# A perceiver layer on one core: half of the sort keys move from VectorE to GpSimd, and ScalarE's row copies are placed anew

## The chip, the cores and the metric

The kernel runs on one core of one Trainium2 chip. The metric is the device time of one execution in microseconds; the time given is the median of three runs.

## The reference

A perceiver layer: cross attention of 4 x 256 query rows to 4 x 4096 context rows (256 columns, 16 heads of 16), then a gated attention with a running sum, then a feed-forward part in 4-bit floating point. What is changed lies in the cross attention, in the focus and the sparsifying of queries and keys:

```python
def _focus(x, f):
    x = jnp.abs(jnp.where(x >= 0, x, 0.01 * x)) + 1e-6
    nrm = x.mean(axis=-1, keepdims=True)
    return jax.nn.softmax(jnp.log(x) * f, axis=-1) * nrm

def _topk_sparsify(x):               # rows of 16 values, one head each
    _, idx = jax.lax.top_k(jnp.abs(x), 11)
    return x * mask_of(idx)          # the other 5 become 0
...
q, k = _focus(q @ Wq.T, f), _focus(k @ Wk.T, f)
qh, kh = _topk_sparsify(heads(q)), _topk_sparsify(heads(k))
z_inv = einsum('bnd,bd->bn', qh, kh.mean(axis=1)) + 1e-6
kv = einsum('bnc,bnd->bcd', kh / 64, vh / 64)
y = einsum('bnc,bcd->bnd', qh, kv) / z_inv[..., None]
```

Every row of 256 values is thus projected, made positive, raised to a power, normalised, and in each of its 16 heads the 5 smallest of 16 values are set to zero. Ties go by position, as top_k has them.

## The kernel before

**Groups.** The rows are worked on in groups of 1024: 128 partitions by T = 8 tiles of 256 columns, 2048 elements in a partition. Group 0 is the queries, groups 1 to 16 are the context, four for each batch. After group 0 the work goes by pairs of groups: `pairs_of_groups` (L298) calls `pair(a, last)` for a = 1, 3, ... 15 on each of three engines; b = a + 1 is the second group of the pair, c = a + 2 and d = a + 3 are the groups of the next pair. Each engine runs its own written-out order of steps, and semaphores tie them.

**One group's way.** TensorE transposes the context rows (`context_turn` L779, `transpose_quad` L739, matmuls on L745) in four quads of two tiles. ScalarE copies each quad out of PSUM to `rows_T` (`rows_to_sbuf` L471, activation on L422), and TensorE projects it (`project` L764, L772). ScalarE's `lift` (L461, L467) makes the value positive and adds up the row; two tiles each time, four times a group. The columns lie by position first: columns 16j to 16j + 15 are position j of the 16 heads. VectorE's `make_keys` (L1200, L1203) makes a sort key of each lifted value: an integer operation clears the lowest four bits and writes the order of the position there, with `key_and` and `key_xor` (L1179 to L1185). Then it finds the fifth smallest key of each head by a network of minima and maxima: `compare_pairs` (L1224), `sort_fours` (L1238, which also gives the row maximum `rowmax`, L1250), `find_fifths` (L1257). `make_mask` (L1281, L1286) compares all keys with it. Meanwhile ScalarE takes the logarithm of the lifted values in place (`logarithms` L480, L484), which must wait until the keys are made, and the exponentials (`exponentials` L486, L501), which need the row maximum. VectorE multiplies by the mask (`apply_mask` L1215, L1219) and makes the row scale (L1221); ScalarE scales (`scale_rows` L507, L513), and TensorE sums products with the context rows (`sum_group` L858, L866).

**Buffers.** `focus_words` holds six planes of a group: two lifted (also the logarithms), two key planes, two of exponentials; each is taken by group number modulo 2. So the keys of group c go where those of group a were, and may not before `make_mask(a)` is done. There is one `mask`. TensorE has two banks for transposed quads and four for projections.

**Order of VectorE in a pair** (L1317): `compare_pairs(a)`, `sort_fours(a)`, `make_keys(b)`, `compare_pairs(b)`, `sort_fours(b)`, `find_fifths` of both, `make_mask(a)`, `inverse_sums(a)`, `apply_mask(a)`, `make_mask(b)`, `make_keys(c)`, `inverse_sums(b)`, `apply_mask(b)`. The last pair has an order of its own, with `make_keys(b)` in the same place.

**Order of ScalarE in a pair** (L524): logarithms of a, copies 0 and 1 of c, exponentials of a, logarithms of b, (in every second pair `save_sums`), then exponentials of b in two halves with the row copies and lifts of c and d between and behind them, `scale_rows(a)` ahead of the last two lifts of d, and `scale_rows(b)` last.

**Order of TensorE in a pair** (L873): turns 0 and 1 of c, the sums of the group before a, then projections and turns of c and d by turns, then the sums of a.

**GpSimd** (L357) makes constants at the start, a maximum over partitions at L389, and splits the biases of the gated attention (L403, L405, L408). After that it has nothing to do. **SP** issues the context loads (L312).

Of the kernel before, what the change touches and what calls it, by code (L numbers as in the profile page):

```python
# [18 lines left out]
P = 128  # L19
F32 = mybir.dt.float32  # L20
BF16 = mybir.dt.bfloat16
I32 = mybir.dt.int32
I16 = mybir.dt.int16
ALU = mybir.AluOpType
# [5 lines left out]
HEADS, HD = 16, 16  # L30
HIDDEN = 1024
# [13 lines left out]
FP4_MAX, FP8_MAX = 6.0, 448.0  # L45
TINY = 1e-20
# [17 lines left out]
def perceiver_layer(nc, x, ctx, Wq, Wk, Wv, Wp, focus, W_qkv, b_qkv, W_gate, b_gate,  # L64
# [9 lines left out]
    with es:  # L74
# [48 lines left out]
        key_xor = sb("key_xor", [P, D], I32)  # L123
# [9 lines left out]
        key_and = sb("key_and", [P, 1], I32)  # L133
        key_flip = sb("key_flip", [P, 1], I32)
        key_base = sb("key_base", [P, 1], I32)
# [100 lines left out]
        keyed = sem("keyed")  # L236
        logs_done = sem("logs_done")
# [58 lines left out]
        LAST_QUAD = AFTER_QUAD + len(TAIL_QUADS)  # L296

# [112 lines left out]

        @block.scalar
        def _(act):
# [67 lines left out]
            def logarithms(n, s):  # L480
                act.wait_ge(lifted_ready, PAIRS * n + PAIRS)
                act.wait_ge(keyed, n + 1)
                logs = lifted[(s + 1) % 2]
                act.activation(logs, logs, ACT.Ln, bias=EPS).then_inc(logs_done, 1)  # L484
# [39 lines left out]
            def pair(a, last):  # L524
# [18 lines left out]
                else:  # L543
                    exponentials(b, at(b), FORE_TILES)
                    rows_to_sbuf(c, 2)
                    lift(c, 0, at(c))
                    exponentials(b, at(b), HIND_TILES)
                    rows_to_sbuf(c, 3)
                    lift(c, 1, at(c))
                    lift(c, 2, at(c))  # L550
                    lift(c, 3, at(c))
                    rows_to_sbuf(d, 0)
# [508 lines left out]
        def _(dve):  # L1061
# [110 lines left out]
            for t in range(T):  # L1172
# [6 lines left out]
            step(dve.tensor_scalar(key_and[:, :], ff[:, :], 0.0, -float(HD), ALU.not_equal, ALU.mult))  # L1179
            step(dve.tensor_scalar(key_flip[:, :], ff[:, :], 0.0, -1.0, ALU.is_lt, ALU.mult))  # L1180
            then(dve.tensor_scalar(key_base[:, :], ff[:, :], 0.0, -1.0, ALU.is_equal, ALU.mult))
            step(dve.tensor_scalar(key_flip[:, :], key_flip[:, :], 0x7FFFFFF0, None, ALU.bitwise_and))
            then(dve.tensor_scalar(key_base[:, :], key_base[:, :], 0x3F800000, None, ALU.bitwise_and))
            then(dve.tensor_scalar(key_xor[:, :], order[:, :], key_base[:, 0:1], key_flip[:, 0:1],
                                   ALU.bitwise_xor, ALU.bitwise_xor))  # L1185
            step(dve.tensor_reduce(same_head[:, :], head_pick[:, :, :].rearrange("p m h -> p h m"), AX.X, ALU.add))
            def weight_max(w):
# [426 lines left out]
```

## Time and profile before

| what | value |
|---|---|
| median of 3 runs | 490.59 us (490.52 to 491.7) |
| the profiled execution | 490.7 us |
| its span, first to last instruction | 488.9 us |
| mean granted TensorE clock | 0.936 |
| busy: VectorE (DVE) / TensorE (PE) / ScalarE (ACT) / GpSimd (POOL) | 448.5 / 388.1 / 356.0 / 15.3 us |
| chain that ended last: VectorE / TensorE / issue / ScalarE | 68% / 16% / 9% / 4% |

In the profile DVE is VectorE, PE is TensorE's matmuls and PEld its weight loads, ACT is ScalarE, POOL is GpSimd. Times are microseconds from the start of the span; L numbers are lines of the kernel. A matmul's end is modelled, and the spans of GpSimd are rough. Groups of instructions name their output and input by the kernel's tensors; planes that lie in `focus_words` all carry that name.

### The profile page before, as it was taken

The page shows a single profiled execution, that of the slowest core. Times are in us where ns is not written, and L with a number is a line of the kernel's source. Part 1 is how long each engine was busy: PE and PEld are TensorE (multiplying, and loading weights), DVE is VectorE, ACT ScalarE, POOL GpSimd, SP SyncE. Part 2 cuts the span into 40 slices and gives each one's busy share as a digit, 9 for nine tenths or more (in the row PEclk, how much of TensorE's full clock was granted, in tenths as well). Part 3 has the DMA queues.
Part 4 walks back from the last instruction along what each step waited for, and adds up shares of the span by engine and source line. Part 5 has one row for each costly group of instructions (what it writes and reads, how often), then busy time and mean ns, then how long its engine had stood idle before and what let it go on. Part 6 is the DMA issues. An engine that isn't in the chain of part 4 may idle for free.

```text
span 488.9 us, 5944 instructions
## 1 busy us (share of the span) xinstructions
PE 388.1 (79%) x1877; PEld 300.9 (62%) x1880; DVE 448.5 (92%) x684; ACT 356.0 (73%) x937; POOL 15.3 (3%) x32
## 2 busy tenths in 40 slices
PE   1997749998988988988988898955999799554563
PEld 1876537777877877877777777855875345112232
DVE  4798999999999999999999999999988687989994
ACT  2569986897897887897887897855459466656643
POOL 4001420000000000000000000000000000000000
PEclk9998879999999999999999999985999999669976
DMA  7952000220220220220220220230200000000001
GB/s 235 359 181 86 0 1 1 87 86 2 86 86 2 86 87 1 87 86 1 87 86 1 86 86 1 62 112 0 87 0 0 1 1 1 0 0 0 23 21 43
DMA packets 27102, 27.65 MB, mean 57 GB/s; under 512 B 1216, under 2 KB 26816, under 8 KB 27072
## 3 DMA queue, kind: packets, MB, share of 16 engines
q1 hardware_dynamic: 26704, 27.27, 17.4%
q8 instruction: 15, 0.25, 0.2%
q14 instruction: 15, 0.12, 0.1%
q0 software_dynamic: 224, 0.01, 0.0%
q10 hardware_dynamic: 144, 0.00, 0.0%
HBM read 26.22 MB, written 1.05 MB: 56 GB/s over the span
## 4 chain that ended last, share of the span: by engine, by line
DVE 68%; PE 16%; issue 9%; ACT 4%; DMA 1%; SPq 0%; ACTq 0%
DVE focus_words L1219 8%; DVE focus_words L1203 8%; PE bank L944 5%; DVE sorted L1242 4%; DVE level L1228 4%; DVE level L1229 4%; DVE merge L1255 4%; DVE sorted L1243 4%; PE bank L772 3%; DVE sorted L1147 3%; DVE amax L1116 2%; DVE sorted L1248 2%; DVE sorted L1247 2%; DVE keymax L1245 2%; DVE merge L1253 2%
## 5 line engine op out<-in xcount | busy, mean ns | idle before, releaser
L772 PE MATMUL bank<-WkT,rows_T 128*128 128x256 f32 x512 | 127.0, 395 | 33.1 <-ACT rows_T L422 33.1
L772 PEld LDWEIGHTS bank<-WkT,rows_T 128*128 128x128 f32 x512 | 96.7, 197 | 50.6 <-ACT rows_T L422 38.8
L866 PE MATMUL bank<-ctx_words,focus_words 128*128 128x257 f32 x512 | 115.7, 384 | 4.9 <-ACT focus_words L513 4.9
L866 PEld LDWEIGHTS bank<-ctx_words,focus_words 128*128 128x128 f32 x512 | 99.8, 198 | 18.3 <-ACT focus_words L513 7.7
L501 ACT ACTIVATE focus_words<-focus_words,shift,ff 128x256 f32<-128x256 f32 x136 | 79.9, 591 | 0.6
L467 ACT ACTIVATE focus_words<-bank 128x256 f32<-128x256 f32 x136 | 50.0, 378 | 26.7 <-PE bank L772 26.7
L513 ACT ACTIVATE focus_words<-focus_words,row_scale 128x256 f32<-128x256 f32 x136 | 56.2, 508 | 11.6 <-DVE row_scale L1221 11.6
L422 ACT ACTIVATE rows_T<-bank 128x512 f32<-128x512 f32 x78 | 44.4, 595 | 23.5 <-PE bank L745 23.5
L1203 DVE SCALAR_TENSOR_TENSOR focus_words<-focus_words,key_and,key_xor 128x2048 int32<-128x2048 int32 x17 | 39.9, 2345 | 1.9 <-ACT focus_words L467 1.9
L745 PE MATMUL bank<-ident,ctx_words 128*128 128x128 f32 x256 | 38.4, 279 | 3.5 <-DMA ctx_words<-in_ctx_dram 2.9
L1286 DVE TENSOR_TENSOR mask<-focus_words,fifth 128x2048 bf16<-128x2048 f32 x17 | 39.0, 2292 | 0.5
L745 PEld LDWEIGHTS bank<-ident,ctx_words 128*128 128x128 f32 x256 | 31.6, 144 | 11.4 <-DMA ctx_words<-in_ctx_dram 5.2
L1219 DVE TENSOR_TENSOR focus_words<-focus_words,mask 128x2048 f32<-128x2048 f32 x17 | 38.6, 2268 | 0.0
L484 ACT ACTIVATE focus_words<-focus_words 128x2048 f32<-128x2048 f32 x17 | 32.4, 1909 | 0.0
L944 PE MATMUL bank<-WattT,rows_T 128*128 128x512 f32 x64 | 30.8, 603 | 0.0
L981 PE MATMUL bank<-gateT,focus_words 128*128 128x512 bf16 x30 | 13.4, 537 | 20.9 <-DVE ctx_words L1386 10.7
L467 ACT ACTIVATION_READ_ACCUMULATOR focus_words<-bank 128x1 f32 x136 | 27.7, 204 | 0.0
L501 ACT ACTIVATION_READ_ACCUMULATOR focus_words<-focus_words,shift,ff 128x1 f32 x136 | 25.8, 190 | 0.0
L745 PE MATMUL bank<-ident,focus_words 128*128 128x128 f32 x80 | 13.4, 307 | 12.2 <-DMA focus_words<-in_L_xattn_Wk_dram 9.5
L1242 DVE TENSOR_TENSOR sorted<-level 128x1024 f32<-128x1024 f32 x17 | 20.8, 1224 | 0.5
L646 ACT ACTIVATE ctx_words<-bank,out_scale 128x512 f32<-128x512 f32 x16 | 10.9, 686 | 14.3 <-PE bank L981 14.3
L1228 DVE TENSOR_TENSOR level<-focus_words 128x1024 f32<-128x1024 f32 x17 | 20.8, 1222 | 0.3
(187 smaller groups left out, 581.5 us busy)
## 6 DMA issues: line engine op xcount, KB each, us to landing
ctx_words<-in_ctx_dram SPq DMA_DIRECT2D x32, 512.0 KB, 3.9
ctx_words<-in_L_ffn_gate_w_dram SPq DMA_DIRECT2D x2, 1024.0 KB, 8.3
ctx_words<-in_L_ffn_up_w_dram SPq DMA_DIRECT2D x2, 1024.0 KB, 8.7
xs<-in_x_dram SPq DMA_DIRECT2D x4, 256.0 KB, 5.0
ctx_words<-in_L_ffn_down_w_dram SPq DMA_DIRECT2D x2, 512.0 KB, 9.5
ctx_words<-in_L_ffn_down_w_dram SPq DMA_DIRECT2D x1, 1024.0 KB, 4.8
out_dram<-xs SPq DMA_DIRECT2D x4, 256.0 KB, 2.1
focus_words<-in_L_attn_W_qkv_dram SPq DMA_DIRECT2D x1, 768.0 KB, 8.3
```

What stands on the lines that cost most here:

```text
L422: ins = act.activation(dst, src, ACT.Copy)
L467: ins = act.activation(lifted[(s + 1) % 2][:, t, :], proj_bank[m][:, (t % 2) * D:(t % 2 + 1) * D], ACT.Prelu, bias=NOT_ZERO, alpha=-0.01, ...
L501: ins = act.activation(expo[slot][:, t, :], lifted[slot][:, t, :], ACT.Exp, bias=shift[:, t:t + 1], scale=ff[:, 0:1], accum_out=exp_sum[:, ...
L513: ins = act.activation(expo[slot][:, t, :], expo[slot][:, t, :], ACT.Identity, scale=row_scale[:, slot, t:t + 1])
L745: ins = pe.transpose(quad_bank[par][:, b * P:(b + 1) * P], src, ident[:, :])
L772: ins = pe.matmul(proj_bank[m][:, t * D:(t + 1) * D], rows_T[:, m % 2, 2 * t + k, :], WT[:, k, :], start=(k == 0), stop=(k == KT - 1))
L866: ins = pe.matmul(sum_bank[k][:, 0:GW], heads_half(expo[slot][:, t, :], k), ctx_ring[:, s, t, :], start=(s == 0 and t == 0), stop=(s == PE ...
L944: pe.matmul(dst, TAIL_ROWS[f"xhat{t // 2}"][:, 2 * (t % 2) + k, :], WattT[:, k, half * 512:(half + 1) * 512], start=(k == 0), stop=False)
L1203: dve.scalar_tensor_tensor(out=key[n % 2].bitcast(I32), in0=lifted[(s + 1) % 2].bitcast(I32), scalar=key_and[:, 0:1], in1=key_xor[:, :].re ...
L1219: tt(expo[slot], expo[slot], mask[:, :, :], ALU.mult).then_inc(masked_ready, 1)
L1228: step(tt(level1[:, :, 0:4:2, :], k4[:, :, 0:4:2, :], k4[:, :, 1:4:2, :], ALU.min))
L1242: step(tt(sorted4[:, :, 2:4, :], level1[:, :, 0:2, :], level1[:, :, 2:4, :], ALU.max))
```

## The change

`make_keys` makes keys by floating-point arithmetic: the lifted value (or, where the exponent is zero, a large constant) times 1 + order x 2^-22, negative where the exponent is negative. From group 3 on VectorE makes only the keys of positions 8 to 15 (columns 128 to 255). GpSimd makes those of positions 0 to 7, one tensor_scalar of 128 partitions x 8 tiles x 16 columns for each position, since the factor is a scalar of the partition. It waits for the lifts of group n and for the mask of group n - 2. VectorE's `compare_pairs` and ScalarE's `logarithms` wait for both halves. On VectorE `make_keys(c)` moves behind `apply_mask(b)`; masks are counted by a semaphore of their own. On ScalarE three row copies move forward in the order of a pair.

```diff
+POOL_POSITIONS, POOL_FROM = 8, 3
+KEY_TOP, ORDER_STEP = 3e38, 2.0 ** -22
...
+        def pool_keys_of(n):
+            return POOL_POSITIONS * max(n + 1 - POOL_FROM, 0)
...
         def _(pool):
...
+            pool.wait_ge(key_consts_ready, 1)
+            for n in range(POOL_FROM, CGROUPS + 1):
+                pool.wait_ge(lifted_ready, PAIRS * n + PAIRS)
+                pool.wait_ge(mask_made, n - 1)
+                for j in range(POOL_POSITIONS):
+                    cols = slice(j * HEADS, (j + 1) * HEADS)
+                    pool.tensor_scalar(key[n % 2][:, :, cols], lifted[n % 2][:, :, cols],
+                                       key_floor[:, 0:1], key_step[:, j * HEADS:j * HEADS + 1],
+                                       ALU.max, ALU.mult).then_inc(pool_keyed, 1)
...
             def logarithms(n, s):
                 act.wait_ge(lifted_ready, PAIRS * n + PAIRS)
                 act.wait_ge(keyed, n + 1)
+                if n >= POOL_FROM:
+                    act.wait_ge(pool_keyed, pool_keys_of(n))
...
                 else:
+                    rows_to_sbuf(c, 2)
                     exponentials(b, at(b), FORE_TILES)
-                    rows_to_sbuf(c, 2)
+                    rows_to_sbuf(c, 3)
                     lift(c, 0, at(c))
                     exponentials(b, at(b), HIND_TILES)
-                    rows_to_sbuf(c, 3)
                     lift(c, 1, at(c))
                     lift(c, 2, at(c))
+                    rows_to_sbuf(d, 0)
                     lift(c, 3, at(c))
-                    rows_to_sbuf(d, 0)
                     rows_to_sbuf(d, 1)
...
-            step(dve.tensor_scalar(key_and[:, :], ff[:, :], 0.0, -float(HD), ALU.not_equal, ALU.mult))
-            step(dve.tensor_scalar(key_flip[:, :], ff[:, :], 0.0, -1.0, ALU.is_lt, ALU.mult))
-            then(dve.tensor_scalar(key_base[:, :], ff[:, :], 0.0, -1.0, ALU.is_equal, ALU.mult))
-            step(dve.tensor_scalar(key_flip[:, :], key_flip[:, :], 0x7FFFFFF0, None, ALU.bitwise_and))
-            then(dve.tensor_scalar(key_base[:, :], key_base[:, :], 0x3F800000, None, ALU.bitwise_and))
-            then(dve.tensor_scalar(key_xor[:, :], order[:, :], key_base[:, 0:1], key_flip[:, 0:1],
-                                   ALU.bitwise_xor, ALU.bitwise_xor))
+            step(dve.tensor_scalar(key_floor[:, :], ff[:, :], 0.0, KEY_TOP, ALU.is_equal, ALU.mult))
+            step(dve.tensor_scalar(key_sign[:, :], ff[:, :], 0.0, -2.0, ALU.is_lt, ALU.mult))
+            settle()
+            then(dve.tensor_scalar(key_sign[:, :], key_sign[:, :], 1.0, None, ALU.add))
+            step(dve.tensor_scalar(key_step[:, :], order[:, :], ORDER_STEP, key_sign[:, 0:1], ALU.mult, ALU.add))
...
+            dve.wait_ge(vstep, done[0])
+            dve.sem_inc(key_consts_ready, 1)
...
             def make_keys(n, s):
 
                 dve.wait_ge(lifted_ready, PAIRS * n + PAIRS)
+                cols = slice(POOL_POSITIONS * HEADS if n >= POOL_FROM else 0, D)
+                order_of = key_step[:, cols]
                 dve.scalar_tensor_tensor(
-                    out=key[n % 2].bitcast(I32), in0=lifted[(s + 1) % 2].bitcast(I32), scalar=key_and[:, 0:1],
-                    in1=key_xor[:, :].rearrange("p (o c) -> p o c", o=1).broadcast_to([P, T, D]),
-                    op0=ALU.bitwise_and, op1=ALU.bitwise_xor).then_inc(keyed, 1)
+                    out=key[n % 2][:, :, cols], in0=lifted[(s + 1) % 2][:, :, cols],
+                    scalar=key_floor[:, 0:1],
+                    in1=order_of.rearrange("p (o c) -> p o c", o=1).broadcast_to([P, T, order_of.shape[1]]),
+                    op0=ALU.max, op1=ALU.mult).then_inc(keyed, 1)
...
-            def apply_mask(n, s, since_mask, since_sums):
+            def apply_mask(n, s, since_sums):
                 slot = (s + 1) % 2
-                settle(but=since_mask)
+                dve.wait_ge(mask_made, n + 1)
...
             def compare_pairs(n):
                 dve.wait_ge(keyed, n + 1)
+                if n >= POOL_FROM:
+                    dve.wait_ge(pool_keyed, pool_keys_of(n))
...
-                dve.tensor_scalar(rowmax[:, slot, :].bitcast(I32), keymax[:, :].bitcast(I32), -HD, key_flip[:, 0:1],
-                                  ALU.bitwise_and, ALU.bitwise_xor).then_inc(rowmax_ready, 1)
+                dve.tensor_scalar(rowmax[:, slot, :], keymax[:, :], key_sign[:, 0:1], None, ALU.mult).then_inc(rowmax_ready, 1)
...
                 make_mask(b)
+                inverse_sums(b, at(b))
+                apply_mask(b, at(b), 0)
                 if not last:
                     make_keys(c, at(c))
-                inverse_sums(b, at(b))
-                apply_mask(b, at(b), 1, 0)
```

## Rows read from the trace of the kernel before

**Rows 1.** The page, part 1: busy time, share of the span, instructions of each engine.
```profile
PE 388.1 (79%) x1877; PEld 300.9 (62%) x1880; DVE 448.5 (92%) x684; ACT 356.0 (73%) x937; POOL 15.3 (3%) x32
```

**Rows 2.** Windows, one pass over a pair: stretch, length, busy by engine, clock, DMA share.
```profile
85.65:122.56 36.91, 32.99 (x162) 28.06 (x162) 36.68 (x45) 31.74 (x100) 0.00 (x0) 1.00 0.19 58
```

**Rows 3.** Timeline of TensorE: start, duration, line, operation, idle before and its releaser.
```profile
86.55 7.22 PE L866 MATMUL bank<-ctx_words,focus_words 128*128 128x257 f32 x32 [0.70 <-ACT focus_words L513]
...
103.80 0.60 PE L745 MATMUL bank<-ident,ctx_words 128*128 128x128 f32 x4
...
113.52 1.99 PE L772 MATMUL bank<-WkT,rows_T 128*128 128x256 f32 x8 [0.98 <-ACT rows_T L422]
...
122.27 2.01 PE L866 MATMUL bank<-ctx_words,focus_words 128*128 128x257 f32 x8 [0.70 <-ACT focus_words L513]
```

**Rows 4.** Waits, 196.3 to 307.1 us: total, times, longest.
```profile
ACT lnmax L492 <- DVE rowmax L1250: 2.2, 3, 1.2
```

**Rows 5.** Groups by form: count, busy us, mean ns, idle before.
```profile
L1203 DVE SCALAR_TENSOR_TENSOR focus_words<-focus_words,key_and,key_xor 128x2048 int32<-128x2048 int32 x17 | 39.9, 2345 | 1.9 <-ACT focus_words L467 1.9
```

**Rows 6.** Timeline of VectorE over the seam of two pairs.
```profile
184.77 2.29 DVE L1286 TENSOR_TENSOR mask<-focus_words,fifth 128x2048 bf16<-128x2048 f32 x1
...
187.10 2.29 DVE L1219 TENSOR_TENSOR focus_words<-focus_words,mask 128x2048 f32<-128x2048 f32 x1
...
191.70 2.35 DVE L1203 SCALAR_TENSOR_TENSOR focus_words<-focus_words,key_and,key_xor 128x2048 int32<-128x2048 int32 x1
...
193.96 0.20 DVE L1213 RECIPROCAL rcp_sum<-exp_sum 128x8 f32<-128x8 f32 x1
...
200.97 0.68 DVE L1245 TENSOR_REDUCE keymax<-sorted 128x8 f32<-128x512 f32 x1
...
204.64 2.34 DVE L1203 SCALAR_TENSOR_TENSOR focus_words<-focus_words,key_and,key_xor 128x2048 int32<-128x2048 int32 x1
...
207.02 1.22 DVE L1228 TENSOR_TENSOR level<-focus_words 128x1024 f32<-128x1024 f32 x1
...
208.16 1.22 DVE L1229 TENSOR_TENSOR level<-focus_words 128x1024 f32<-128x1024 f32 x1
```

**Rows 7.** Timeline of GpSimd, 56 to 62 us.
```profile
56.56 0.57 POOL L405 TENSOR_TENSOR bias_left<-bias_col,bias_split 128x8 f32<-128x8 f32 x1 [6.64 <-issue]
57.20 2.18 POOL L403 CAST bias_split<-bias_left 128x8 bf16<-128x8 f32 x1
59.46 1.19 POOL L405 TENSOR_TENSOR bias_left<-bias_left,bias_split 128x8 f32<-128x8 f32 x1
60.71 1.07 POOL L403 CAST bias_split<-bias_left 128x8 bf16<-128x8 f32 x1
```

**Rows 8.** Timeline of VectorE, the same stretch.
```profile
56.98 2.35 DVE L1203 SCALAR_TENSOR_TENSOR focus_words<-focus_words,key_and,key_xor 128x2048 int32<-128x2048 int32 x1
59.36 1.22 DVE L1228 TENSOR_TENSOR level<-focus_words 128x1024 f32<-128x1024 f32 x1
60.51 1.22 DVE L1229 TENSOR_TENSOR level<-focus_words 128x1024 f32<-128x1024 f32 x1
```

**Rows 9.** Timeline of GpSimd at the start, VectorE reading little.
```profile
3.76 0.22 POOL L367 MEMSET ident_b<- 128x128 bf16 x1
3.90 0.22 POOL L368 MEMSET ones<- 128x128 f32 x1
...
5.15 0.29 POOL L373 TENSOR_SCALAR_AFFINE_SELECT ident_b<-ident_b 128x128 bf16<-128x128 bf16 x1
5.40 0.29 POOL L376 TENSOR_SCALAR_AFFINE_SELECT upto<-upto 128x128 f32<-128x128 f32 x1
...
6.51 0.21 POOL L386 MEMSET ctx_words<- 128x8 f32 x4
```

**Rows 10.** Timeline of ScalarE.
```profile
103.01 0.21 ACT L492 ACTIVATE lnmax<-rowmax 128x8 f32<-128x8 f32 x1
...
197.00 0.39 ACT L467 ACTIVATE focus_words<-bank 128x256 f32<-128x256 f32 x1
```

More of the change, by code:

```diff
@@ L122, in perceiver_layer @@
         order = sb("order", [P, D], I32)
-        key_xor = sb("key_xor", [P, D], I32)
+        key_step = sb("key_step", [P, D])
         head_pick = sb("head_pick", [P, HD, HALF_HEADS])
@@ L132, in perceiver_layer @@
         ff_neg = sb("ff_neg", [P, 1])
-        key_and = sb("key_and", [P, 1], I32)
-        key_flip = sb("key_flip", [P, 1], I32)
-        key_base = sb("key_base", [P, 1], I32)
+        key_floor = sb("key_floor", [P, 1])
+        key_sign = sb("key_sign", [P, 1])
         in_scale = sb("in_scale", [P, 2])
@@ L236, in perceiver_layer @@
         keyed = sem("keyed")
+        pool_keyed = sem("pool_keyed")
+        key_consts_ready = sem("key_consts_ready")
+        mask_made = sem("mask_made")
         logs_done = sem("logs_done")
@@ L1285, in make_mask @@
                     dve.wait_ge(masked_ready, n)
-                step(tt(mask[:, :, :].rearrange("p t (j h) -> p t j h", h=HEADS),
-                        key[n % 2].rearrange("p t (j h) -> p t j h", h=HEADS),
-                        fifth[:, of_pair(n), :].rearrange("p t (o h) -> p t o h", o=1).broadcast_to([P, T, HD, HEADS]),
-                        ALU.is_gt))
+                tt(mask[:, :, :].rearrange("p t (j h) -> p t j h", h=HEADS),
+                   key[n % 2].rearrange("p t (j h) -> p t j h", h=HEADS),
+                   fifth[:, of_pair(n), :].rearrange("p t (o h) -> p t o h", o=1).broadcast_to([P, T, HD, HEADS]),
+                   ALU.is_gt).then_inc(mask_made, 1)
             make_keys(0, -1)
@@ L1297, in _ @@
             inverse_sums(0, -1)
-            apply_mask(0, -1, 1, 0)
+            apply_mask(0, -1, 0)
             dve.wait_ge(w_max_taken, 3)
@@ L1332, in pair @@
                 inverse_sums(a, at(a))
-                apply_mask(a, at(a), 1, 0)
+                apply_mask(a, at(a), 0)
                 if last:
```

## The prediction, made before the changed kernel ran

> **What bounds the kernel now.** The page comes first: VectorE is busy 92% of the span, TensorE 79%, ScalarE 73%, and GpSimd hardly at all [rows 1]. The busy time by stretch shows where that matters. The six middle passes over a pair of groups, all like the one shown, last 36.9 us each, and VectorE works 36.7 of them, TensorE 33.0, ScalarE 31.7 [rows 2]. So in the loop VectorE is the bound, by a small margin, and a cut in its work is worth its full length only until another loop closes.
>
> How near is that other loop? It is the one between TensorE and ScalarE: transpose, row copy, projection, lift, scaling, sums. One pass of it was not held by VectorE: the sums of the first group of two successive pairs start at 86.55 and 122.27 us [rows 3], 35.7 us apart. In the passes from 196 to 307 us ScalarE waits for VectorE's row maximum three times, 2.2 us in total [rows 4], so there the two loops run within about 1 us of each other. The ceiling on what VectorE's relief can give is thus 36.9 - 35.7 = 1.2 us a pair, unless the ScalarE order is bettered too.
>
> **Keys on VectorE, the gain.** A key instruction takes 2.35 us [rows 5]; back to back it occupies 2.26 us (191.70 to 193.96, the start of the small reciprocal behind it) [rows 6]. Half the columns is the shape of a 128x1024 comparison, spaced 1.14 us [rows 6]. Maximum and multiply take the place of two bit operations in the same instruction form; I cost that at nothing. 14 groups (3 to 16) are halved: 14 x 1.13 = **15.8 us off VectorE**. Groups 0 to 2 stay whole. The constants differ by a few instructions of 0.1 us before the first context arrives, which nothing waits for.
>
> **Keys on GpSimd, the price.** Eight instructions a group, 112 in all, each 128x128. If they ran beside VectorE at no cost the whole 15.8 us would stand. The trace says they don't run beside it. At 57.20 GpSimd begins a cast of 8 columns, which takes 2.18 us; it ends at 59.38, just after VectorE's key instruction, from 56.98 to 59.33. The next ones begin at 59.46 and 60.71, take 1.19 and 1.07 us, and end 0.05 to 0.07 us behind VectorE's comparisons (60.58, 61.73) [rows 7, 8]. These VectorE instructions read two tensors. So a GpSimd instruction that reads waits out such a VectorE instruction, and gets its turn at the seam to the next.
>
> What does VectorE lose at the seam? With 8 columns, next to nothing: its starts are 2.38 and 1.15 us apart there [rows 8], and 2.38 and 1.14 us at the same places of a pair with GpSimd silent [rows 6]. With 128 columns it must be more. From below: 0.01 us, the tiny one. From above: 0.3 us, the whole span of an affine_select of 128 columns, which reads and writes; its spacing is 0.25 us. Memsets of 128 columns are spaced 0.14 us, four of 8 columns fit in 0.21 us [rows 9], that is some 0.04 us each. The 120 further columns cost about 0.10 us; with the 0.01 us of the tiny one that makes 0.11, and I take 0.12 us, because a maximum and a multiply on one input are nearer to the memset than to the select. Both ends stay for the range.
>
> How many seams are paid for? **Second group of a pair** (b): its last lift runs from 197.00 us, and VectorE reaches the next key instruction at 204.64 [rows 6, 10]. Between them lies the reduction at 200.97 (0.60 us, one input), behind which I let three of the eight pass free. Five are paid, and the eight are done in time. **First group of the next pair** (c): GpSimd must wait for the mask of group a, for the key buffer is the same; that mask starts at 184.77 and ends near 187.0. From there VectorE has two applications, a mask, two reciprocals, two row scales and half a key instruction before it compares [rows 6]. That gives some six seams, of which I pay five and let the one under the reciprocal pass; two GpSimd instructions are left over, and VectorE stands still for them: 2 x 0.2 us, and 0.1 us for the signal, 0.5 us. That wait is new, on VectorE, with everything behind it; ScalarE's logarithms wait for the same signal but stand behind its last lift at 197.00 us and the scaling of b [rows 10], so they are not held up. So: b 5 x 0.12 = 0.6, c 0.6 + 0.5 = 1.1 us. Seven of each: 7 x 1.7 = **11.9 us given back**.
>
> There is also a first call. GpSimd's first tensor_tensor stood behind 6.64 us of issue [rows 7]. Does tensor_scalar pay the like? If the load comes before the waits, nothing; if after, it delays group 3 by perhaps 1.5 us. I take 0.5.
>
> Key making of c now follows the application of b's mask. ScalarE scales b before it takes c's logarithms, so nothing is later for it; and b's application, over at about 196.3 us even before, is earlier now than ScalarE can use it, which is at its last lift until 197.4 [rows 6, 10]: zero. Without that cover it would be a gain. The added semaphore waits on VectorE are for its own work or for long finished work: under 0.1 us a pair, in the 0.5 above. Row maximum by a multiply: same form and size, zero.
>
> **Row copies on ScalarE.** The third copy of c now stands ahead of b's exponentials. ScalarE was ready at 103.01 us, and that quad's transpose only starts at 103.80, so it waits some 1.3 us there; then the copies of c and the first of d come sooner. I walked the new order through with the durations of this pass: the first copy of d, which TensorE waits for 0.98 us until 113.52 [rows 3, 10], lands 0.3 us earlier. The loop of TensorE and ScalarE shrinks from 35.7 to about 35.4 us. While VectorE is the bound, it is worth 0, and a wait placed badly there costs nothing until it has used up the 1.2 us that loop has in hand.
>
> **Sum.** Period: 36.9 - 2.26 + 0.6 + 1.1 = 36.3 us, above 35.4, so VectorE still bounds. -15.8 + 11.9 + 0.5 = -3.4 us. The profiled execution took 490.7 us (span 488.9, 1.8 around it), the median is 490.59: **487.3 us**.
>
> **Rival 1, the seam costs little, and the other loop closes (chance 0.25).** For: 8 columns cost 0.01 us, and VectorE's instructions overlap by 0.08 us at a seam anyway. Against: 128 columns must be read. Six pairs at 35.4 instead of 36.9 us give 9.0, the first and last pair 1.1 each: 490.7 - 11.2 + 0.5 = 480 us. More than that needs ScalarE's order to be worth more than the 0.3 us I find.
>
> **Rival 2, slower: GpSimd holds VectorE for its whole instruction (chance 0.27).** Place: the same seams. Price: 0.25 us, the spacing of the select; 70 seams x 0.25 = 17.5, the idle wait for c grows to 0.8 us, 7 x 0.8 = 5.6, and 0.5: 23.6 against 15.8 saved, so 498.5 us. With the idle waits as in the forecast (7 x 0.5 = 3.5 us) it decides from (15.8 - 0.5 - 3.5) / 70 = 0.17 us a seam. The Trainium skill speaks for this one: SBUF — State Buffer, Who interferes with whom, has GpSimd and a VectorE instruction with two SBUF inputs contend by an exclusive lock, held by whoever issues first for the whole instruction, not a sharing of bandwidth. The casts that end with VectorE's instructions agree [rows 7, 8]; what a 128-column instruction holds no row shows.
>
> **Rival 3, the division doesn't help because GpSimd is late (0.05).** If it gets fewer seams than I count, more of the eight stand bare before c's comparison; at four instead of two, 7 x 0.5 us more: 490.5 us, no change.
>
> **How the numbers follow.** The forecast has 0.43; seam prices of 0.08 to 0.17 us make its own range 484.5 to 490.8. The predicted time is its 487.3. The range 479 to 498 takes in rival 1 and nearly all of rival 2. A measurement of this kernel can tell about 0.3%, 1.5 us, from no change. Faster: rival 1, and 0.24 of the forecast, 0.49. Same: 0.15 of the forecast and 0.02 of rival 3, 0.17. Slower: rival 2, 0.04 of the forecast, 0.03 of rival 3: 0.34.
>
> **What would show it.** VectorE's key instruction at 1.2 us for groups 3 to 16; 112 GpSimd instructions, many ending with a VectorE instruction; starts on VectorE spaced 0.1 to 0.15 us wider at seams where GpSimd is active; a wait of VectorE for GpSimd of 0.3 to 0.7 us before c's comparison, seven times; pairs of 36.3 us. Pairs of 35.4 us with VectorE idle on lifts would show rival 1, seams 0.25 us wider rival 2. The prediction is wrong at its root if GpSimd's instructions take a microsecond each while VectorE is silent, or if ScalarE's new order moves TensorE's loop by more than 1 us either way.

## The result, and the profile after

The changed kernel takes 523.85 us (median of six executions), the kernel before 491.67 us in the same runs: ratio 1.0661, 95% interval 1.0643 to 1.0680. It is slower by 6.6%, where 487.3 us and a gain were forecast. (One of its six executions took 985 us; it is left out of the ratio, and nothing in this study explains it.) The profiled execution took 524.0 us, its span is 522.3 us.

The page, part 1, of the changed kernel:

```profile
PE 402.6 (77%) x1877; PEld 310.7 (59%) x1880; DVE 439.9 (84%) x682; ACT 357.1 (68%) x937; POOL 188.6 (36%) x144
```

Against [rows 1] VectorE works 8.6 us less, and its share has fallen from 92 to 84%: it is no longer the bound. The same pass over a pair as in [rows 2], by windows:

```profile
200.65:242.48 41.83, 34.19 (x161) 28.95 (x160) 35.47 (x44) 31.27 (x98) 24.60 (x16) 0.96 0.16 51
```

A pair takes 41.8 us in place of 36.9. VectorE is busy 35.5 of them and stands idle for over 6. Groups of instructions, count, busy, mean, idle before:

```profile
L425 POOL TENSOR_SCALAR focus_words<-focus_words,key_floor,key_step 128x128 f32<-128x128 f32 x112 | 173.6, 1562 | 116.0 <-DVE mask L1310 116.0
L1253 DVE TENSOR_TENSOR level<-focus_words 128x1024 f32<-128x1024 f32 x17 | 22.0, 1297 | 40.9 <-POOL focus_words L425 40.8
L1225 DVE SCALAR_TENSOR_TENSOR focus_words<-focus_words,key_floor,key_step 128x1024 f32<-128x1024 f32 x14 | 19.5, 1390 | 0.0
```

VectorE's key instruction fell from 2.35 [rows 5] to 1.39 us, where the forecast had 1.2; with no GpSimd instruction beside it the half key takes 1.28 us (in the one-multiply run below). But a GpSimd instruction takes 1.56 us in the mean, and the first comparison of a group waits 40.8 us in all for GpSimd. The waits of the whole kernel show who is held up in turn:

```profile
POOL focus_words L425 <- DVE mask L1310: 116.0, 7, 17.2
ACT lnmax L512 <- DVE rowmax L1275: 46.7, 15, 4.3
DVE level L1253 <- POOL focus_words L425: 40.8, 13, 3.9
ACT focus_words L504 <- POOL focus_words L425: 6.8, 8, 1.5
```

And one seam of two pairs, VectorE first, where [rows 6] had no idle time at all:

```profile
202.98 2.29 DVE L1242 TENSOR_TENSOR focus_words<-focus_words,mask 128x2048 f32<-128x2048 f32 x1
...
205.38 2.36 DVE L1310 TENSOR_TENSOR mask<-focus_words,fifth 128x2048 bf16<-128x2048 f32 x1
...
207.77 2.42 DVE L1242 TENSOR_TENSOR focus_words<-focus_words,mask 128x2048 f32<-128x2048 f32 x1
210.11 0.15 DVE L1244 SCALAR_TENSOR_TENSOR row_scale<-abs_sum,rcp_sum 128x8 f32<-128x8 f32 x1
210.19 1.40 DVE L1225 SCALAR_TENSOR_TENSOR focus_words<-focus_words,key_floor,key_step 128x1024 f32<-128x1024 f32 x1
215.44 1.40 DVE L1253 TENSOR_TENSOR level<-focus_words 128x1024 f32<-128x1024 f32 x1 [3.85 <-POOL focus_words L425]
...
224.12 1.39 DVE L1225 SCALAR_TENSOR_TENSOR focus_words<-focus_words,key_floor,key_step 128x1024 f32<-128x1024 f32 x1
227.82 1.22 DVE L1253 TENSOR_TENSOR level<-focus_words 128x1024 f32<-128x1024 f32 x1 [2.31 <-POOL focus_words L425]
```

GpSimd in the same stretch, one line from each of eight narrow windows; these are the eight instructions of group c:

```profile
203.12 2.82 POOL L425 TENSOR_SCALAR focus_words<-focus_words,key_floor,key_step 128x128 f32<-128x128 f32 x1 [17.23 <-DVE mask L1310]
205.92 2.47 POOL L425 TENSOR_SCALAR focus_words<-focus_words,key_floor,key_step 128x128 f32<-128x128 f32 x1
208.38 2.47 POOL L425 TENSOR_SCALAR focus_words<-focus_words,key_floor,key_step 128x128 f32<-128x128 f32 x1
210.84 1.41 POOL L425 TENSOR_SCALAR focus_words<-focus_words,key_floor,key_step 128x128 f32<-128x128 f32 x1
212.23 0.78 POOL L425 TENSOR_SCALAR focus_words<-focus_words,key_floor,key_step 128x128 f32<-128x128 f32 x1
213.00 0.79 POOL L425 TENSOR_SCALAR focus_words<-focus_words,key_floor,key_step 128x128 f32<-128x128 f32 x1
213.78 0.79 POOL L425 TENSOR_SCALAR focus_words<-focus_words,key_floor,key_step 128x128 f32<-128x128 f32 x1
214.55 0.79 POOL L425 TENSOR_SCALAR focus_words<-focus_words,key_floor,key_step 128x128 f32<-128x128 f32 x1
```

While VectorE works, an instruction of GpSimd takes about 2.5 us here, since it waits for a turn. The first four end at 205.94, 208.39, 210.85 and 212.25, each 0.65 to 0.67 us behind the end of a long VectorE instruction with two inputs (205.27, 207.74, 210.19, 211.59). While VectorE stands still (from 211.6), the last four follow each other in 0.78 us. Among VectorE's 1.2 us comparisons after 215.44, GpSimd's starts stand 2.45 us apart (216.09, 218.54, 220.98), two comparisons each. The eight of group c begin at 203.12, as forecast right behind the mask of group a, and end at 215.3; VectorE needed them at 211.6. So it waits 0.66 us for the fourth, four times 0.78 us for the others, and for the signal: 3.85 us.

The account of a pair: 37.09 us (all keys on VectorE, measured below), less 2.13 for the halved keys (twice 2.345 - 1.28), plus 3.85 and 2.31 of waiting, makes 41.1. The other 0.7 us are put down to VectorE's instructions that became longer beside GpSimd, 0.05 us for each of the 16. The busy time of the whole kernel gives the same: 449.2 us with all keys on VectorE, less 14.9 for 14 halved keys, is 434.3, and 439.9 was measured, 5.6 us for 112 instructions.

### The profile page after: what moved, and what is told of

It reads as the page before. It is cut to its first block, busy times and chain, and to the rows that moved or that the text cites. A ratio compares the mean times of both kernels' runs of the same rounds, so it can differ in the third digit from the quotient of the medians.

```text
span 522.3 us, 6083 instructions
## 1 busy us (share of the span) xinstructions
PE 402.6 (77%) x1877; PEld 310.7 (59%) x1880; DVE 439.9 (84%) x682; ACT 357.1 (68%) x937; POOL 188.6 (36%) x144
## 4 chain that ended last, share of the span: by engine, by line
DVE 44%; POOL 30%; PE 15%; issue 4%; ACT 4%; DMA 1%; SPq 0%; POOLq 0%; DVEq 0%; ACTq 0%
POOL focus_words L425 30%; PE bank L964 4%; DVE mask L1310 3%; PE bank L792 3%; DVE sorted L1167 2%; DVE sorted L1267 2%; DVE level L1254 2%; DVE merge L1279 2%; DVE sorted L1268 2%; DVE level L1253 2%; DVE amax L1136 2%; PE bank L765 2%; PE bank L1001 2%; DVE rank L1290 1%; PE bank L886 1%
## 5 line engine op out<-in xcount | busy, mean ns | idle before, releaser
L425 POOL TENSOR_SCALAR focus_words<-focus_words,key_floor,key_step 128x128 f32<-128x128 f32 x112 | 173.6, 1562 | 116.0 <-DVE mask L1310 116.0
L792 PE MATMUL bank<-WkT,rows_T 128*128 128x256 f32 x512 | 137.7, 420 | 48.0 <-ACT rows_T L440 47.8
L792 PEld LDWEIGHTS bank<-WkT,rows_T 128*128 128x128 f32 x512 | 103.4, 210 | 68.8 <-ACT rows_T L440 54.6
L1253 DVE TENSOR_TENSOR level<-focus_words 128x1024 f32<-128x1024 f32 x17 | 22.0, 1297 | 40.9 <-POOL focus_words L425 40.8
L765 PE MATMUL bank<-ident,ctx_words 128*128 128x128 f32 x256 | 40.0, 287 | 3.6 <-DMA ctx_words<-in_ctx_dram 3.0
L765 PEld LDWEIGHTS bank<-ident,ctx_words 128*128 128x128 f32 x256 | 33.2, 150 | 12.4 <-DMA ctx_words<-in_ctx_dram 5.4
L1242 DVE TENSOR_TENSOR focus_words<-focus_words,mask 128x2048 f32<-128x2048 f32 x17 | 39.8, 2343 | 0.0
L512 ACT ACTIVATE lnmax<-rowmax 128x8 f32<-128x8 f32 x17 | 3.6, 212 | 46.7 <-DVE rowmax L1275 46.7
L1225 DVE SCALAR_TENSOR_TENSOR focus_words<-focus_words,key_floor,key_step 128x1024 f32<-128x1024 f32 (+1 forms) x17 | 26.5, 1559 | 3.1 <-ACT focus_words L485 3.1
```

The lines of the kernel that those rows point to most:

```text
L425: pool.tensor_scalar(key[n % 2][:, :, cols], lifted[n % 2][:, :, cols], key_floor[:, 0:1], key_step[:, j * HEADS:j * HEADS + 1], ALU.max, ...
L765: ins = pe.transpose(quad_bank[par][:, b * P:(b + 1) * P], src, ident[:, :])
L792: ins = pe.matmul(proj_bank[m][:, t * D:(t + 1) * D], rows_T[:, m % 2, 2 * t + k, :], WT[:, k, :], start=(k == 0), stop=(k == KT - 1))
L1242: tt(expo[slot], expo[slot], mask[:, :, :], ALU.mult).then_inc(masked_ready, 1)
```

## The experiments

The theory after the result, called G: GpSimd is late, VectorE's seams cost little. Rivals: the row copies placed anew hurt (A); the floating-point keys, or their new place in VectorE's order, hurt (B).

### Without GpSimd's keys

```diff
-POOL_POSITIONS, POOL_FROM = 8, 3
+POOL_POSITIONS, POOL_FROM = 8, 99
...
-            for n in range(POOL_FROM, CGROUPS + 1):
-                ...
```

> The changed kernel with all keys made by VectorE again (floating-point keys, the key making of c behind the application of b's mask, and the new placing of the row copies all kept). Theory G (GpSimd's eight instructions a group are late and VectorE stands for them, some 6 us a pair): the whole loss goes, 490 to 492 us, pairs of 36.9 us. Rival A (the row copies placed anew hurt): stays above 505 us. Rival B (the floating-point keys or their place in the order hurt VectorE): stays above 500 us, with longer key instructions than 2.35 us.

Measured: 493.12 us, ratio 1.0033 (1.0023 to 1.0044), pairs of 37.09 us. The loss is gone but for 1.5 us: G holds, A and B fall as causes of it. A key instruction takes 2.34 us, as the integer one did.

The second takes the row copies back as well:

```diff
+                    exponentials(b, at(b), FORE_TILES)
                     rows_to_sbuf(c, 2)
-                    exponentials(b, at(b), FORE_TILES)
-                    rows_to_sbuf(c, 3)
                     lift(c, 0, at(c))
                     exponentials(b, at(b), HIND_TILES)
+                    rows_to_sbuf(c, 3)
                     lift(c, 1, at(c))
                     lift(c, 2, at(c))
-                    rows_to_sbuf(d, 0)
                     lift(c, 3, at(c))
+                    rows_to_sbuf(d, 0)
```

> As the kernel without GpSimd's keys, and the row copies back in their old places. Theory G, with VectorE as the bound: no difference from that kernel beyond 1.5 us, for the copies lie in the loop that has about 1 us a pair in hand. Rival A: 490 us here and above 505 us there.

Measured: 493.46 us, ratio 1.0038 (1.0025 to 1.0050), pairs of 37.09 us. No difference, as expected while VectorE bounds.

The third keeps the new copies and puts the key making of c back:

```diff
                 make_mask(b)
+                if not last:
+                    make_keys(c, at(c))
                 inverse_sums(b, at(b))
                 apply_mask(b, at(b), 0)
-                if not last:
-                    make_keys(c, at(c))
```

> The kernel without GpSimd's keys, with the key making of group c put back ahead of the inverse sums and the application of b's mask. That kernel's pairs are 37.09 us against 36.91 before. If the new place costs the 0.18 us (the comparison now waits for the key instruction right behind it, and the application for its mask), pairs are 36.9 us here and the time is that of before within 0.5 us, 491 to 492 us. If the floating-point keys cost it, pairs stay at 37.1 us and the time at 493 us.

Measured: 491.97 us, ratio 1.0010 (0.9998 to 1.0021), pairs of 36.92 us. So the remaining 0.17 us a pair were the new place, and the floating-point keys cost nothing.

### What a GpSimd instruction takes alone

Seven forms at the start of the kernel before, VectorE waiting until they are done (shortened: `out[8x16]` stands for 16 columns of each of the 8 tiles, `s` for two pointer scalars, that is, factors read from a tensor and not written into the instruction as immediates):

```diff
+                probed(pool.tensor_scalar(out[8x16], in[8x16], s[:, 0:1], s[:, 1:2], ALU.max, ALU.mult))
+                probed(pool.tensor_scalar(out[8x16], in[8x16], 0.0, 1.0, ALU.max, ALU.mult))
+                probed(pool.tensor_scalar(out[8x16], in[8x16], s[:, 0:1], None, ALU.mult))
+                probed(pool.tensor_scalar(out[128], in[128], s[:, 0:1], s[:, 1:2], ALU.max, ALU.mult))
+                probed(pool.tensor_scalar(out[8x128], in[8x128], s[:, 0:1], s[:, 1:2], ALU.max, ALU.mult))
+                probed(pool.tensor_tensor(out[8x128], in[8x128], in[128 broadcast], ALU.mult))
+                probed(pool.tensor_tensor(out[8x16], in[8x16], in[16 broadcast], ALU.mult))
```

> The kernel before, with seven forms of GpSimd instruction run twice at the start while VectorE waits, each waited for before the next: tensor_scalar of 8x16 columns with two pointer scalars, with two immediates, with one pointer and one operation, of 128 columns in one piece with two pointers, of 1024 columns with two pointers, tensor_tensor of 1024 and of 8x16 columns. The first should take the 0.78 us that it took in the changed kernel while VectorE stood still. If the pointers are what costs, the immediates take 0.3 us or less; if the short pieces of 16 columns, the one piece takes 0.3; if the second operation, the single one takes half. If the cost goes by the column, 1024 columns take 6 us; if by the instruction, 1.5 to 2 us.

The first round, GpSimd's timeline; the lines L402 to L408 are the forms in this order:

```profile
7.88 0.82 POOL L402 TENSOR_SCALAR rank<-merge,probe_s 128x128 f32<-128x128 f32 x1
8.78 0.64 POOL L403 TENSOR_SCALAR rank<-merge 128x128 f32<-128x128 f32 x1
9.52 0.61 POOL L404 TENSOR_SCALAR rank<-merge,probe_s 128x128 f32<-128x128 f32 x1
10.24 0.80 POOL L405 TENSOR_SCALAR rank<-merge,probe_s 128x128 f32<-128x128 f32 x1
11.13 3.77 POOL L406 TENSOR_SCALAR rank<-merge,probe_s 128x1024 f32<-128x1024 f32 x1
14.99 2.28 POOL L407 TENSOR_TENSOR rank<-merge 128x1024 f32<-128x1024 f32 x1
17.35 0.45 POOL L408 TENSOR_TENSOR rank<-merge 128x128 f32<-128x128 f32 x1
```

The changed kernel's form takes 0.80 us alone. Pieces of 16 columns are not the reason (one piece: 0.80), the two pointers are a fifth of it (0.64 with immediates). With one pointer and one operation it is 0.61; how much of that saving is the operation's wasn't measured by itself. By size it is (3.77 - 0.80) / 896 = 3.3 ns a column and 0.38 us an instruction. A memset of the same size, from which the forecast took its price, spans 0.22 us [rows 9]. The kernel as a whole took 513.1 us in its single execution, VectorE having waited for the probe.

### What it takes from VectorE

VectorE makes all keys, and GpSimd does the same work on a weight tensor into a side buffer; nobody waits for it:

```diff
-                    pool.tensor_scalar(key[n % 2][:, :, cols], lifted[n % 2][:, :, cols],
+                    pool.tensor_scalar(side[:, :, (j % 4) * HEADS:(j % 4 + 1) * HEADS], side_in[:, :, cols],
                                        key_floor[:, 0:1], key_step[:, j * HEADS:j * HEADS + 1],
                                        ALU.max, ALU.mult).then_inc(pool_keyed, 1)
```

> VectorE makes all keys, and GpSimd carries out the same 112 instructions on a weight tensor into a side buffer; nobody waits for them. What is left of the loss is what GpSimd's reading takes from VectorE at the seams. Theory G: busy time of VectorE rose by about 1 us for 16 instructions in the changed kernel, so 7 x 1.1 = 7 to 8 us slower than before, 498 to 500 us. Rival C (a GpSimd instruction shuts VectorE out for its whole length, 0.78 us): 112 x 0.78 = 87 us, 570 us or more. Rival D (the seams cost nothing): 491 us. If GpSimd needs two turns for each instruction, the starts in its timeline stand two of VectorE's instructions apart.

Measured: 502.9 us, ratio 1.0232 (1.0216 to 1.0247); pairs of 38.54 us. That is 9.8 us over the kernel without GpSimd's keys. VectorE's busy time is 459.1 us against 449.2: 9.9 us for 112 instructions, 0.09 us each. This is more than the 7 to 8 us that G expected. Rival C, that VectorE is shut out for 0.78 us, falls; so does D, that the seams cost nothing.

The same with immediates (`0.0, 1.0` for the two pointers):

> As GpSimd on the side, with the two pointer scalars replaced by the immediates 0.0 and 1.0. Alone such an instruction takes 0.64 us instead of 0.80. If GpSimd needs one turn at VectorE's seams for the pointers and another for the tensor (theory G2), the mean length beside VectorE falls from 2.25 us to some 1.2 to 1.5 us, and VectorE's busy time falls by about a third to a half of the 9.9 us it gained (it was 459.1 against 449.2), 497 to 499 us. If the turns have nothing to do with the pointers, the mean stays above 2.0 us and the time at 502 to 503 us.

Measured: 497.64 us, ratio 1.0125 (1.0110 to 1.0140). GpSimd's group in the two kernels, pointers first:

```profile
L429 POOL TENSOR_SCALAR side<-WattT,key_floor,key_step 128x128 f32<-128x128 f32 x112 | 250.3, 2247 | 28.6 <-issue 17.3 <-DVE mask L1314 11.4
```
```profile
L429 POOL TENSOR_SCALAR side<-WattT 128x128 f32<-128x128 f32 x112 | 164.0, 1492 | 98.1 <-issue 85.5 <-DVE mask L1313 12.6
```

Alone the immediates save 0.16 us, beside VectorE 0.76 us, and VectorE's busy time is 454.8 us, 0.05 us for each in place of 0.09. This is what a second turn for the pointers would do (theory G2). It fits the pace in the changed kernel (one instruction to two of VectorE's comparisons, and one to each long instruction of the masks and applications, where a reciprocal or row scale of 0.2 us stands between and makes a second seam), but that the pointers take a turn of their own is inferred from lengths, not seen.

Two-input instructions of 8x16 columns on the side:

> GpSimd on the side with 112 tensor_tensor multiplies of 8x16 columns (0.45 us each alone) in place of the tensor_scalars, nobody waits. The 1024-column multiply kept VectorE out for 2.1 us, nearly its whole length, the 128-column tensor_scalar for 0.09 us of 0.80. Theory L1 (a two-input instruction holds VectorE for its reading, whatever its size, 2.0 ns a column): 0.25 us or more each, VectorE's busy time up by 28 us or more against 449.2, 516 us or above. Theory L2 (what fits at one go is read quickly, and only long instructions hold): near the tensor_scalar's price of 0.09, at most 0.15 us each, 500 to 508 us.

Measured: 514.22 us, ratio 1.0462 (1.0441 to 1.0483), VectorE busy 470.9 us: 21.7 / 112 = 0.19 us each. Neither theory's number; the shorter instruction (0.45 us alone, 1.55 us in the mean here) takes twice as much from VectorE as the longer tensor_scalar. That it reads two tensors is the likely reason, and isn't shown by itself.

### Versions of the share

**Four positions** of the changed kernel's form (`POOL_POSITIONS = 4`):

> The changed kernel with 4 positions by GpSimd in place of 8. VectorE makes 192 of 256 columns: 14 x 0.56 = 7.9 us less work; 56 instructions at 0.09 us each on VectorE give back 5.0, and the other parts of the change cost 1.5 us. Theory G: four instructions of some 2.2 us fit nearly into the 8 us that VectorE has before it compares group c, so its waits for GpSimd fall from 41 us to under 7 us in all: 489 to 496 us. If the seams or anything else than the wait were the loss, it would lie half way, near 508 us.

Measured: 495.83 us, ratio 1.0085 (1.0070 to 1.0101); VectorE's waits for GpSimd fall from 40.8 to 6.0 us. With half of GpSimd's work gone, nearly all of the waiting goes, and 28 of the 32 us with it. Had the loss been the price at the seams, it would have halved.

**One multiply** a group (shortened; it leaves out the maximum with the floor):

```diff
-                for j in range(POOL_POSITIONS):
-                    ...
+                pool.tensor_tensor(key[n % 2][:, :, 0:128], lifted[n % 2][:, :, 0:128],
+                                   key_step[:, 0:128] broadcast over the tiles, ALU.mult).then_inc(pool_keyed, 1)
```

> GpSimd makes its half of the keys by one tensor_tensor multiply of 1024 columns a group instead of eight tensor_scalars; it leaves out the maximum with the floor, which is 0 here because the exponent isn't zero. Alone such an instruction took 2.28 us against 8 x 0.80. Theory G: it is done long before VectorE compares, 14 x 1.13 = 15.8 us come off VectorE, 14 seams give back little, the other parts of the change cost 1.5, and then TensorE's and ScalarE's loop bounds at 35.4 us a pair: 478 to 484 us. Rival C2 (a reading instruction of GpSimd shuts VectorE out for its whole length, 2.28 us): 14 x 2.2 = 31 us given back, 505 to 509 us. In between (VectorE slowed while both read): 485 to 495 us.

Measured: 507.6 us, ratio 1.0324 (1.0306 to 1.0343). Here my theory failed and the rival (C2) held. GpSimd and VectorE around a seam:

```profile
193.78 4.40 POOL L423 TENSOR_TENSOR focus_words<-focus_words,key_step 128x1024 f32<-128x1024 f32 x1 [26.60 <-DVE mask L1308]
...
203.12 3.12 POOL L423 TENSOR_TENSOR focus_words<-focus_words,key_step 128x1024 f32<-128x1024 f32 x1 [4.93 <-ACT focus_words L483]
```
```profile
195.88 2.33 DVE L1242 SCALAR_TENSOR_TENSOR row_scale<-abs_sum,rcp_sum 128x8 f32<-128x8 f32 x1
...
202.73 1.28 DVE L1223 SCALAR_TENSOR_TENSOR focus_words<-focus_words,key_floor,key_step 128x1024 f32<-128x1024 f32 x1
204.04 3.28 DVE L1251 TENSOR_TENSOR level<-focus_words 128x1024 f32<-128x1024 f32 x1
```

The multiply waits for the application to end at 195.96, and then VectorE's row scale, 0.16 us elsewhere, takes 2.33; at the next, a comparison of 1.22 takes 3.28. Each costs VectorE 2.1 to 2.2 us, nearly the 2.28 that the multiply takes alone. A pair is then 37.09 - 2.13 + 2.17 + 2.06 = 39.2 us, and 39.06 was measured. With the old copies (the second diff above):

> As the one multiply, with the row copies in their old places. If the loop of TensorE and ScalarE bounds there, the old placing costs 0.3 us a pair by my walk through the order, some 2 us; if VectorE still bounds, no difference beyond 1.5 us.

Measured: 507.45 us, ratio 1.0336 (1.0313 to 1.0359). No difference.

**Four and six immediates** (`POOL_POSITIONS` 4 and 6), with the new row copies and the key making of c back in its old place:

```diff
-                    pool.tensor_scalar(..., key_floor[:, 0:1], key_step[:, j * HEADS:j * HEADS + 1],
-                                       ALU.max, ALU.mult).then_inc(pool_keyed, 1)
+                    pool.tensor_scalar(..., 1.0 + (HD - 1 - j) * ORDER_STEP, None, ALU.mult).then_inc(pool_keyed, 1)
```

> GpSimd makes 4 of 16 positions, each by one multiply with an immediate factor (this leaves out the floor and the sign, which matter only where the exponent is zero or negative); the key making of c is back in its old place, the new row copies stay. VectorE saves 14 x 0.56 = 7.9 us; 56 instructions at 0.05 us, the price of the immediates on the side, give back 2.8; four of about 1.3 us are done before VectorE compares. Pairs of 36.2 us, 486 to 488 us, faster than before by 1%. If GpSimd still comes late, 489 to 492 us.

> As with four, but 6 of 16 positions. Without waits for GpSimd: 11.8 us saved, 84 x 0.05 = 4.2 given back, 483 to 485 us, pairs of 35.8 us. But six instructions of 1.3 to 1.46 us beside VectorE are 8 to 9 us, more than the 7 to 8 us that it has for group c: I expect it to stand 0.5 to 1 us a pair there, 487 to 491 us, no better than with four.

Measured: four 489.87 us, ratio 0.9962 (0.9949 to 0.9976); six 493.94 us, ratio 1.0049 (1.0035 to 1.0064). With six VectorE waits 9.2 us for GpSimd in all, 1.31 us in each pair and always ahead of group c; it was more than I expected. With four it is 3.7 us, and the gain came out smaller than forecast: the first pairs are 36.5 to 36.6 us, the last three 37.0. Of the shortfall 0.6 us lies in the keys: one of 1536 columns takes 1.83 us, 0.52 less than a whole one and not 0.56. In the pairs of 37.0 us the clock of TensorE and the lifts may come in, which the next two runs take up.

**Four immediates and the changed kernel, each with the old row copies:**

> As four immediates, with the row copies in their old places. If the new placing costs TensorE's clock (granted 0.95 in the loop) and with it the loop of TensorE and ScalarE, the clock is 1.00 here, the pairs are 36.4 us throughout, and the time is 486 to 488 us against 489.9. If the placing is worth nothing, 489.5 to 490.5 us. If it is the gain of 0.3 us a pair that I walked through, slower than with the new copies by 1 to 2 us.

> The changed kernel with the row copies alone put back. Theory G: GpSimd bounds the pairs from the mask of group a on, so the copies are nearly worth nothing: 522 to 526 us, pairs of 41.8 us. If lifted values that come late through the slower clock hold GpSimd up, 515 us or less.

Measured: 489.2 us, ratio 0.9954 (0.9939 to 0.9968), and 523.54 us, ratio 1.0659 (1.0640 to 1.0678). One stretch by windows, four immediates with the new copies and then with the old:

```profile
237.60:274.50 36.90, 33.23 (x159) 28.57 (x158) 35.85 (x44) 30.11 (x94) 8.92 (x8) 0.95 0.19 58
```
```profile
237.60:274.50 36.90, 32.90 (x163) 28.12 (x162) 36.38 (x45) 30.95 (x95) 13.90 (x10) 1.00 0.19 59
```

The granted clock is back at 1.00 (the higher of its two levels throughout), and the pairs are 36.5 us. The time itself differs by 0.7 us, and the intervals overlap; 486 to 488 us was not reached. In the changed kernel the copies are worth nothing. What the new placing does is seen in TensorE's timeline of the two kernels without GpSimd's keys, which differ in nothing but the copies, first with the new ones, then with the old:

```profile
181.82 1.99 PE L783 MATMUL bank<-WkT,rows_T 128*128 128x256 f32 x8 [0.62 <-ACT rows_T L431]
...
186.80 1.99 PE L783 MATMUL bank<-WkT,rows_T 128*128 128x256 f32 x8 [2.55 <-ACT rows_T L431]
```
```profile
181.11 1.99 PE L783 MATMUL bank<-WkT,rows_T 128*128 128x256 f32 x8 [1.28 <-ACT rows_T L431]
...
184.65 2.00 PE L783 MATMUL bank<-WkT,rows_T 128*128 128x256 f32 x8 [1.10 <-ACT rows_T L431]
...
188.05 2.00 PE L783 MATMUL bank<-WkT,rows_T 128*128 128x256 f32 x8 [0.98 <-ACT rows_T L431]
```

Three waits of 1.0 to 1.3 us have become one of 2.55 and one of 0.62. In six stretches of 36.9 us from 90 us on, the granted clock is 0.95 in four and 1.00 in two with the new copies, and 1.00 in all six with the old; these two kernels take the same time all the same, 493.1 and 493.5 us.

**Three positions for each first group, six for each second**, old copies, immediates:

```diff
+        def pool_positions(n):
+            return 3 if n % 2 else 6
```

> As four immediates with old copies, but 3 positions of each first group of a pair (short time ahead of its comparison) and 6 of each second group. Nine instead of eight instructions a pair: VectorE saves 0.14 us more and pays 0.05 more, and the waits ahead of group c's comparison, 0.5 us a pair with four, should go. Pairs of 35.9 to 36.1 us, where the loop of TensorE and ScalarE (35.7) is near: 484.5 to 487 us. If six instructions are late for the second group, waits of VectorE for GpSimd appear in each pair and the time is 487 us or more.

Measured: 485.78 us, ratio 0.9888 (0.9871 to 0.9905). Pairs are 36.09 us, and no wait of VectorE for GpSimd is left; both are as expected. This version beats both kernels, the one before by 1.1%. By windows:

```profile
126.90:163.80 36.90, 33.08 (x165) 28.31 (x164) 36.70 (x46) 31.59 (x99) 11.18 (x11) 1.00 0.19 58
```

VectorE is busy 36.7 of 36.9 us again, as before the change [rows 2]: it is still the bound. These last versions leave out the floor and the sign of the keys, which matter only where the exponent is zero or negative; the added work for these cases isn't in their time.

## Why the prediction was wrong

**What bounded before, and what the keys are worth: right, a little too high.** VectorE bounded. The form with maximum and multiply costs what the bit operations did (pairs of 36.92 against 36.91 us). But half the columns aren't half the time: the half key takes 1.28 us, so a pair saves 2.13 us and not 2.26, and 14 groups 14.9 us in place of 15.8.

**The seam price: right in kind, 0.12 forecast, 0.05 to 0.09 measured** in the mean over all 112. The forecast paid for 70 of them, 8.4 us. It was 5.6 us in the changed kernel, where some run while VectorE stands still, and 9.9 us on the side. That GpSimd's reading waits for VectorE's two-input instructions to end was read from three 8-column instructions [rows 7, 8], and it is what happens.

**The step that failed** is "two GpSimd instructions are left over, and VectorE stands still for them: 2 x 0.2 us". It hid two assumptions. One is the length of a GpSimd instruction. Every row of before had either 8 columns or another operation, and I took a tensor_scalar with two pointers to be nearer to a memset (spaced 0.14 us) than to a select (0.25 us). It is 0.78 us, three times the spacing of the select. The other is that it gets a turn at each seam. Its own 0.78 us become 2.25 us beside VectorE at work; that the pointers take a second turn would explain it, and is inferred. In place of six of the eight instructions of group c, VectorE's work covers three and part of a fourth. Four more stand bare, at 0.78 us each. The eight take 12.2 us, where VectorE's comparison is 8.5 us behind their start, and it waits 3.85 us in place of 0.5.

The second group, which I held to be done in time, waits 2.31 us: its lifts are done at 211.4 us, but GpSimd is at group c until 215.3 and starts on it only then. Together 5.7 us a pair more than forecast, seven times. The forecast 36.3 us a pair and the measured 41.8 differ by 5.5. The prediction also held ScalarE's logarithms not to be held up. They wait 6.8 us for GpSimd in all, and 0.89 of it at the seam shown (its logarithm starts at 215.45 us); what that costs by itself wasn't measured.

**Rival 3 named this mechanism** (GpSimd gets fewer seams, more instructions stand bare), with a chance of 0.05. Its count was four bare instructions, and four there were. But it priced them with the same 0.2 us each and so came to 490.5 us, no change (its own terms, 487.3 + 3.5, add up to 490.8). The range fails for the same reason: it was built on the price at the seam, and the length of the instruction was in it with one value alone. Its upper end of 498 was rival 2's, which isn't the cause here; that "slower" had a chance of 0.34 came mostly from that rival.

**Rival 2**, that GpSimd holds VectorE for its whole instruction, is false for the changed kernel's form (0.05 to 0.09 of 0.78 us), and true for one tensor_tensor of 1024 columns (2.1 of 2.28 us). The Trainium skill's rule (SBUF — State Buffer, Who interferes with whom: an exclusive lock for the whole instruction) thus fits the long instructions of the one-multiply run, where VectorE lost 2.1 to 2.2 us to each, and not the 112 short ones; the measurement decides.

**The first call of 1.5 us** didn't show: in the first pair GpSimd begins at 77.69 us, right behind the mask. **The new place of the key making** was called zero; it costs 0.17 us a pair, 1.2 us in all, of which the 0.5 us for first call and waits covered part. **The row copies** were called worth nothing while VectorE bounds; right within what these runs tell (1.0033 against 1.0038). The 0.3 us that I walked through for the other loop wasn't seen in any run; the walk had not reckoned with the long wait of TensorE that the new order makes, nor with the lower granted clock that went with it.

## What to carry to other kernels

Before work goes to GpSimd, measure the very instruction there: its length alone, and its length beside VectorE. Operation and scalars moved it from 0.22 to 0.82 us for the same 128 columns, so the nearest other operation is no bound. Then hold the sum of the instructions against the time between their last input and their first reader, for each group by itself. Here 8 of 16 positions cost 6.6%. Four left 6.0 us of waiting with pointers and 3.7 or 2.3 us with immediates, and 3 and 6 left none. The price for VectorE's own time has to be measured as well: one 1024-column two-input multiply took 2.1 us from it, eight tensor_scalars for the same columns 0.4 to 0.7.

## What the runs showed of the hardware that I had not expected

- One GpSimd tensor_scalar of 128x128 f32 with two pointer scalars takes 0.80 us alone, with two immediates 0.64, with one pointer and one operation 0.60. A tensor_tensor of the same size takes 0.45 us, and one of 1024 columns 2.28 against 3.77 us for the tensor_scalar. So the two-input instruction, a single multiply, is faster than the tensor_scalar with maximum and multiply.
- Beside VectorE at work these become 2.25 us (pointers) and 1.49 us (immediates), and take 0.09 and 0.05 us from VectorE. A tensor_tensor of 8x16 columns becomes 1.55 us and takes 0.19 us from it, and one of 1024 columns takes 2.1 us. Why a tensor_scalar of 0.80 us costs VectorE 0.09 and a tensor_tensor of 2.28 us nearly its whole length is open; a tensor_scalar of 1024 columns beside VectorE wasn't tried.
- Gathering TensorE's idle time into one wait of 2.55 us a pair and a short one, in place of three of 1.0 to 1.3 us, went with a granted clock of 0.95 in most pairs, where it was 1.00. That the wait is the cause is inferred. The mean over the kernel hardly differs (0.929 and 0.927 without GpSimd's keys, 0.923 and 0.943 for four immediates), and the time by 0.3 and 0.7 us.
